# Column products of a graph-attention kernel: one fp32 table in place of two fp32r parts

## The reference

```
def _gat_conv(x, W, att_src, att_dst, bias, src, dst):      # twice, with W0 and W1
    xw = (x @ W).reshape(N, H, CPH)                          # H = 8 heads of 16 channels
    a_s = jnp.einsum('nhc,hc->nh', xw, att_src)
    a_d = jnp.einsum('nhc,hc->nh', xw, att_dst)
    e = jax.nn.leaky_relu(a_s[src] + a_d[dst], NEG)
    m = jax.ops.segment_max(e, dst, num_segments=N)
    p = jnp.exp(e - m[dst])
    s = jax.ops.segment_sum(p, dst, num_segments=N)
    return jax.ops.segment_sum(xw[src] * (p / s[dst])[:, :, None], dst, num_segments=N).reshape(N, H * CPH) + bias
...
x = x + _L0_gnn_ref(_layernorm(x, axis=-1), edge_index, ...)          # both convolutions side by side, + x, layernorm
x = x + _L0_ffn_ref(_layernorm(x, axis=-1)[None], ...)[0]             # 8 experts, 2 of them for each token
```

## Time and profile before

| what | us |
|---|---|
| time, median of 3 runs | 3142.97 |
| the profiled execution: span from first to last instruction | 3949.4 |
| busy in that span: TensorE / weight loads | 1918.5 / 1741.9 |
| busy: VectorE / ScalarE / GpSimd | 2043.1 / 1578.9 / 1927.4 |
| TensorE at L1299: 4080 MATMUL records | 953.7 busy |

### The profile page before, as it was taken

One profiled execution on the slowest core, in us unless ns is written; L12 is line 12 of the kernel. 1 busy time (PEld: TensorE's weight loads), 2 busy tenths in 40 slices (PEclk: granted clock), 3 DMA queues, 4 the chain that ended last, 5 costly groups with the idle time before them and its releaser, 6 DMA issues.

```text
span 3949.4 us, 38354 instructions
## 1 busy us (share of the span) xinstructions
PE 1918.5 (49%) x10116; PEld 1741.9 (44%) x10117; DVE 2043.1 (52%) x4266; ACT 1578.9 (40%) x2552; POOL 1927.4 (49%) x1920
## 2 busy tenths in 40 slices
PE   4500000134435354453544454545213489999998
PEld 2400000123425344353544453435213389999998
DVE  5465676625527355363554563545687544444443
ACT  4322223315536355453555554445323323333332
POOL 4467657645554555535555555465466612222222
PEclk8755555556767676676677776766655599999999
DMA  8244449313332333323333333233365622222222
GB/s 299 76 117 135 144 161 155 120 42 94 94 94 86 94 93 92 94 80 96 94 96 92 94 92 93 59 99 93 119 220 179 230 42 37 36 36 37 36 36 32
DMA packets 212942, 396.68 MB, mean 100 GB/s; under 512 B 76396, under 2 KB 164785, under 8 KB 206305
## 3 DMA queue, kind: packets, MB, share of 16 engines
q1 hardware_dynamic: 136049, 245.72, 18.4%
q0 software_dynamic: 75664, 149.21, 16.8%
q10 hardware_dynamic: 1120, 0.52, 0.0%
HBM read 203.53 MB, written 191.78 MB: 100 GB/s over the span
## 4 chain that ended last, share of the span: by engine, by line
PE 34%; issue 25%; DVE 16%; DVEq 10%; another core or an unknown queue 8%; ACT 4%; SPq 1%; POOL 1%; DMA 1%; POOLq 0%; ACTq 0%
PE ps L1299 13%; PE ps L1390 9%; PE ps L1396 9%; DVEq L1703 5%; DVE AR L1708 4%; PE ps L1270 1%; ACT onehot L1155 1%; ACT AR L1084 1%; DVEq L1709 1%; DVE AR L1773 1%; POOL AR L882 1%; DVE group_stats L1945 1%; ACT onehot L1159 1%; PE ps L1381 1%
## 5 line engine op out<-in xcount | busy, mean ns | idle before, releaser
L882 POOL DMA_INDIRECT AR<-tables,idx x1443 | 1377.0, 954 | 1095.5 <-DMA state<-AR 620.8
L1299 PE MATMUL ps<-table_parts,onehot 128*128 128x408 f32 (+1 forms) x4080 | 953.7, 388 | 1218.1 <-issue 752.5
L1299 PEld LDWEIGHTS ps<-table_parts,onehot 128*128 128x128 f32 x4080 | 861.9, 221 | 1309.9 <-issue 949.7
L1771 DVE TENSOR_SCALAR AR<-ps,tile_pick 128x136 f32<-128x136 f32 x120 | 35.4, 351 | 991.2 <-PE ps L1299 555.4
L1084 ACT COPY AR<-AR 128x1984 f32<-128x1984 f32 (+3 forms) x110 | 392.0, 3564 | 355.1 <-DVE AR L1708 195.6
L956 POOL DMA_INDIRECT out<-AR,idb x105 | 183.5, 1748 | 597.6 <-issue 560.1
L1708 DVE TENSOR_TENSOR_SCAN AR<-ps,AR 128x512 f32<-128x512 f32 x404 | 454.2, 1197 | 0.0
L1390 PEld LDWEIGHTS ps<-AR 128*128 128x128 f32 x3360 | 393.9, 193 | 6.6 <-DVE AR L2164 1.3
L1390 PE MATMUL ps<-AR 128*128 128x128 f32 x3360 | 394.5, 276 | 0.9 <-DVE AR L2164 0.9
L1701 DVE TENSOR_TENSOR AR<-AR,ps 128x3968 f32<-128x3968 f32 (+1 forms) x51 | 356.7, 6994 | 20.7 <-ACT AR L1103 13.4
L1101 ACT ACTIVATE ps<-AR 128x248 f32<-128x248 f32 (+1 forms) x51 | 19.2, 376 | 702.4 <-DVE AR L1688 411.4
(11 more groups left out here) (345 smaller groups left out, 2352.4 us busy)
## 6 DMA issues: line engine op xcount, KB each, us to landing
state<-AR SPq DMA_DIRECT2D x50, 2232.0 KB
AR<-tables,idx POOLq DMA_INDIRECT x1492
AR<-in_L_ffn_W SPq DMA_DIRECT2D x16, 1024.0 KB
AR<-placed SPq DMA_DIRECT2D x105, 130.0 KB, 2.0
adstart<-room SPq DMA_DIRECT2D x26, 496.0 KB
AR<-adstart SPq DMA_DIRECT2D x50, 248.0 KB
tables<-AR SPq DMA_DIRECT2D x49, 136.0 KB
room<-tables SPq DMA_DIRECT2D x14, 476.0 KB
```

Of the source, the lines that this page charges most:

```text
L882: pool.indirect_dma_start(out=G[s][:, j, 0:ROWT], out_offset=None, in_=table_rows, in_offset=bass.IndirectOffsetOnAxis(ap=idx[:, s, j:j + ...
L1299: return T.matmul(bank[:, 0:z], mark, table_parts[:, k, v * w:v * w + z], start=(a == 0 and k == 0), stop=(a == LEV - 1 and k == PARTS - 1))
```

## The change

The table is kept as plain fp32 in the area that x leaves, and each mark is multiplied with it once, as an fp32 product, so 17 products a column in place of 34. The transfer that reads it goes straight into that area, and so it is issued after all seven groups of x have been stored, when SP comes to batch 8. `split_table` and its semaphore go; ScalarE and TensorE wait for the transfer itself (`degrees_moved_then_table_loaded` at 48), and TensorE also for the second row of fix-ups (`fix_rows_ready` at 2), which reads a PSUM bank that the products write. One of the two buffers of edge codes moves to another place in the same area.

```
-PARTS = 2
-TABLE_AT = 5
-SPLIT_AT = 8
+TABLE_AT = 8
...
-        rounded = mybir.dt.float32r
         part_size = NT * ROWT
-        table_parts = nc.alloc_sbuf_tensor_at("table_parts", [P, PARTS, part_size], rounded, offset=arena_at + 4 * XO, align_bytes=4)
-        onehot = nc.alloc_sbuf_tensor_at("onehot", [P, LEV, PEC * P], rounded, offset=room_at, align_bytes=4)
-        at = FB + PARTS * part_size - NT * D
+        table = AR[:, XO:XO + part_size]
+        onehot = room[:, 0:LEV * PEC * P].rearrange("p (a c) -> p a c", a=LEV)
+        at = FB + 800
...
                     if b == TABLE_AT:
-                        sp.wait_ge(x_rows_stored, 16 * TABLE_AT)
+                        sp.wait_ge(x_rows_stored, 16 * NG)
...
-                        sp.dma_start(staging.rearrange("p (t r) -> p t r", r=ROWT), tab[0].rearrange("(t p) r -> p t r", p=P)).then_inc(degrees_moved_then_table_loaded, 16)
+                        sp.dma_start(table.rearrange("p (t r) -> p t r", r=ROWT), tab[0].rearrange("(t p) r -> p t r", p=P)).then_inc(degrees_moved_then_table_loaded, 16)
...
                 if i == 0:
-                    act.wait_ge(parts_ready, len(SPLITS))
+                    act.wait_ge(degrees_moved_then_table_loaded, 48)
...
-            def product(bank, mark, a, k):
+            def product(bank, mark, a):
...
-                return T.matmul(bank[:, 0:z], mark, table_parts[:, k, v * w:v * w + z], start=(a == 0 and k == 0), stop=(a == LEV - 1 and k == PARTS - 1))
+                return T.matmul(bank[:, 0:z], mark, table[:, v * w:v * w + z], start=(a == 0), stop=(a == LEV - 1))
...
                     for c in range(PEC):
-                        for k in range(PARTS):
-                            mm = product(column_banks[c], onehot[:, a, c * P:(c + 1) * P], a, k)
+                        mm = product(column_banks[c], onehot[:, a, c * P:(c + 1) * P], a)
...
-            pe.wait_ge(parts_ready, len(SPLITS))
+            pe.wait_ge(degrees_moved_then_table_loaded, 48)
+            pe.wait_ge(fix_rows_ready, 2)
...
-            def split_table(k):
...
-                for first, n in SPLITS[k]:
-                    a, z = first * ROWT, (first + n) * ROWT
-                    upper = room[:, part_size:part_size + n * ROWT]
-                    V.tensor_scalar(upper.bitcast(I32), staging[:, a:z].bitcast(I32), UPPER_BITS, None, ALU.bitwise_and)
-                    dd()
-                    V.tensor_copy(table_parts[:, 0, a:z], upper)
-                    last = V.tensor_tensor(table_parts[:, 1, a:z], staging[:, a:z], upper, ALU.subtract)
-                    dd()
-                last.then_inc(parts_ready, 1)
...
             def whole_batch(b, w=L, next_w=L):
-                if SPLIT_AT <= b < SPLIT_AT + len(SPLITS):
-                    split_table(b - SPLIT_AT)
```

More of the change, by code:

```diff
@@ L97 @@
 MIDDLE = float(LEV * P // 2)
-UPPER_BITS = -(1 << 12)
-SPLITS = (((0, 13), (13, 12)), ((25, 12), (37, 12)))
 LEVEL_ORDER = (0, LEV - 1, *range(1, LEV - 1))
@@ L296, in build @@
         columns_taken = sem("columns_taken")
-        parts_ready = sem("parts_ready")
         rows_copied = sem("rows_copied")
@@ L478, in build @@
         degree_rows = share_of.rearrange("p a b c t h -> p (a b c t h)")[0:NT, 0:P]
-        staging = room[:, 0:part_size]
         def repeats(w):
```

## The result

The changed kernel takes 3237.27 us (median of four runs, 3235.08 to 3240.13), the kernel before 3142.74 (four runs, 3141.74 to 3144.03). The medians differ by 94.5 us, a ratio of 1.0301; the ratio on record, formed from the fast runs with a 95% interval, is 1.0308 [1.0296, 1.0321]: slower. The forecast was 3303 us, in a range from 3195 to 3415; direction, mechanism and range held, and the size was 66 us too high.

A forecast was written before the change was run, and what follows sets the result against it. The prediction took GpSimd's gathers to bound the kernel before (34.3 us a batch) and TensorE's burst, pause and clock after (38.3 us): 40 x (38.3 - 34.3) = +160 us on 3143, 3303 us, range 3195 to 3415.

The forecast's parts named there:

- Mechanism: Batches 10 to 49: GpSimd's gathers set the pace before, TensorE's products at a mixed clock after; chance 0.56.
- The burst: TensorE's 102 records a batch at L1299: 33.6 us in fp32, where a free run took 20.76 us.
- The pause: TensorE's wait between bursts while VectorE empties three PSUM banks: 2.99 us, making the cycle 36.6 us at full clock.
- The clock: TensorE behind its pauses: after 9 of 17 it runs at 1.2 GHz and loses 3.2 us, 1.7 us a batch.
- P1: The changed kernel's batch, set by TensorE's burst, pause and clock: 38.3 us, ends 36.6 and 39.8.
- P0: The batch of a timed run before the change, set by GpSimd's gathers: 34.3 us, between 31.7 and 35.0.
- The lower bound: P0's lower end, 31.7 us: all 806.4 us of the profiled execution's excess lost in the 40 batches.
- rival 1: TensorE's clock holds through every pause: P1 36.6, +92 us, 3235 us (3205 to 3267); chance 0.08.
- rival 4: Gathers take 38.3 us or more a batch and hide TensorE's work: not slower, 3131 to 3149 us; chance 0.12.
- The split: Twelve VectorE instructions in two rounds (L1787 to L1790) go: costed at nothing, up to 12 us without the gathers' cover.
- The transfer: 3332 KB move from batch 5 to behind batch 8's store on SP's queue: cost nothing, if late at most some 10 us.
- The stalls: One-at-a-time products at TensorE, 752.5 us of waits before L1299: of the profiled execution alone, following records, not work.

The follow-up runs named there:

- second profile of before: The kernel before, unchanged, profiled once more: 3139.68 us, span 3137.9 us.
- half of the levels: The changed kernel with the column products of odd levels left out (9 of 17 levels stay): 3138.11 us, ratio 0.9981 to the kernel before.
- the spare bank: The changed kernel with a fourth PSUM bank: 3137.68 us, ratio 0.9977 to the kernel before; with the split's twelve VectorE instructions put back, 3140.17 us, 0.9999.
- two columns: 2 columns a batch on TensorE in place of 3: on the changed kernel 3184.52 us, ratio 1.0138; on the kernel before 3190.71 us, ratio 1.0156.
- the earlier trace: The profile of the kernel before that the prediction read; profiled execution 3949.4 us, median of the runs 3143.0 us.
- first profile of before: The kernel before, unchanged, in the profile that the prediction read: execution 3949.4 us, with stalls.
- a fourth column: The kernel before (two fp32r parts) with 4 columns a batch on TensorE in place of 3, the fourth in PSUM bank 0: 3090.71 us, ratio 0.9836.

## Why the prediction was right, and where its size was off

**Mechanism: right.** Gathers before, TensorE's cycle after. The second profile of before shows the gathers without a pause; half of the levels and the spare bank bring the batch back to 34.9 us and no further, two columns give 29 x 1.25 in both kernels. The signs named in the prediction's last part came too: 102 records a batch, VectorE waiting for the products, and GpSimd with 517.9 - 444.8 = 73 us of idle time ahead of gathers that isn't its own issue: 72.7 of it, in 28 waits, end with the stores that free a slot, where the second profile of before has 2.6 in one.

**The burst: right.** 33.84 us against 33.6, the price built from the expert stage. The Trainium skill, FP8 and Floating Point Precision, TensorE Precision Notes, gives a true fp32 product four passes through the array. The trace agrees for fp32: the burst bears out 340 ns for a record of 408 columns, two records a product, and 4 x 408 columns at one a cycle of 2.4 GHz, an estimate, are the same 680 ns. Doubling 20.76 would yet have given 41.5. The burst before was longer than its passes: its start was at the lower clock, and at the full clock a record took 183 ns, with weight loads busy for 14.87 of 15.00 us. In after, weight loads are busy for 773.8 us beside 1394.2 of products. So the likely pace of the burst before was one weight load a record and not the columns; no run moves the weight loads alone.

**The pause: right**, 2.99 us, as in the earlier trace rows. It is what turns a burst that would fit (34.0 a batch with the spare bank) into a cycle that doesn't.

**The clock: a mis-sized term.** I put it at 1.7 us a batch: 9 of 17 pauses, 3.2 us each. It measured 0.84 in the time, 1.02 in the records. The share was about right, 23 of 39 pauses where I had 9 of 17; but the clock mostly stays at the lower level for 2.9 us, not for 6.2 to 6.8, so that a burst mostly loses 35.27 - 33.84 = 1.4 us. Part of this was a misreading of the earlier trace rows: the four windows with a clock of 0.72 hold only 2 x 0.28 x 6.0 = 3.4 us at 1.2 GHz, and just the five near 0.50 stand for 6 us and more. With 1.7 us for the four and 3.2 for the five the term would have been 1.3. The rest was carried over from a kernel with bursts of 20.76 us to one with longer bursts. P1 was 37.67 us over the stage where I had 38.3; from burst to burst at TensorE it was (2107.46 - 670.40)/38 = 37.82, that is 33.84 + 2.99 + 0.99 for the clock.

**P0: a mis-sized term.** I took 34.3 us, between 31.7 and 35.0; it was 34.99, the upper bound. The lower bound had no mechanism: it only let all 806 us be lost in these batches. It was also miscounted: from one batch's largest instruction to another's, the 2072.9 us are 39 periods of 53.2 us and not 40 of 51.8, and the 422.1 us are 10 periods and not 9. By 39 the lower bound is 32.5, and a batch of 35.0 explains 708 of the 806 us in place of 673. The gathers at 1.25 us, in stalled and unstalled stretches alike, were a mechanism, and the batch of 29.3 us is no batch of 28 gathers. The first profile of before shows what it was:

```profile
1190.70:1220.10 29.40, 23.19 (x114) 22.40 (x113) 25.16 (x34) 24.46 (x29) 0.00 (x0) 0.88 0.09 28
```

```profile
1226.46 0.95 POOL L882 DMA_INDIRECT AR<-tables,idx  x1 [52.02 <-DMA state<-AR]
```

In the batch ahead of it, of 29.40 us, GpSimd does nothing. VectorE had stood for 61.17 us, until 1181.90, GpSimd had meanwhile filled all the slots it could and then stood 52.02 us until a store freed one. So VectorE ran these batches from slots filled earlier: 29.3 us is its own pace with a full stock, not that of a batch whose gathers have yet to be issued.

These two terms make 0.69 + 0.63 us a batch, 53 of the 66 us. Of the rest 6.8 us were gained outside the stage (5.2 + 1.6), 2.7 are the one period by which the stretch from batch 10 to batch 49 is shorter than the sum's 40, and 3.4 are the difference between what the profiled spans (97.9) and the medians (94.5) lose. The time lies at rival 1's 3235, but not for its reason: there the clock never fell, and P1 was 36.6. That the two agree is luck. Three small slips changed nothing: the lower ends 3205, 3333 and 3245 come to 2 us more by their own terms, and rival 4's 261 us to 265.

**The split: wrong at nothing.** I costed it at nothing because it comes "between gathers that set the pace", and at up to 12 us for the wait of ScalarE if that cover were gone. The cover itself was what it slows: the split lengthens the gathers by about 6.9 us. Taken out, it gave 5 to 7 us (the spare bank without and with it, ratios of 0.9977 and 0.9999 and gathers 5.2 us apart; the two-column kernels, 6.2 us apart in time and 6.9 in their gathers). The wait of ScalarE was only 5.15 us in the second profile and cost nothing that shows.

**The transfer: nothing, as said.** In after it is issued at 590.39 us, and ScalarE makes its first mark at 626.78 right behind its own work, with no wait for it. The stretch ahead of batch 10 is shorter by 5.2 us in after, against 5 to 7 for the split. VectorE's alternation of 10 us, in which such a cut falls, blurs a difference of that size, and no run moves the transfer alone.

**The stalls: half right.** That they belong to the profiled execution alone, on which the sum rested, held. That they "follow records, not work" did not: after has as many records and no stalls, and so has the kernel before in its second profile. What they follow stays open.

## What to carry to other kernels

Compare, for each engine, a whole cycle of a batch (its work, the pause in which its buffers are emptied, and what the clock takes behind that pause) with the bound that stands now: here a burst of 33.8 us would have fitted under 35.0 and lost by 3 us of pause, which a fourth bank hides. An instruction that lies beside the bounding engine's work isn't free for that reason: look whether the bounding engine's own instructions get longer beside it. And where the bound is one engine's even pace (28 x 1.25 us), simplifying another engine's work doesn't move it, while giving that engine a piece of the bound does: here a fourth column took 50 us off.

## What the runs showed of the hardware

**Some of VectorE's instructions in SBUF lengthen GpSimd's gathers.** 0.94 us becomes 1.38 to 2.55 beside the split's mask, copy and subtract. The Trainium skill, SBUF — State Buffer, SBUF: two separate sides, says that a DMA issued from GpSimd has its descriptors written by GpSimd, and that a VectorE instruction in a mode which takes the port pair shared by the two keeps it from writing them. The trace agrees in that the gathers beside these instructions, and not the one ahead of them at 0.94 us, are longer; which of the three kinds of instruction holds them most wasn't separated. Two instructions of one size in after's timeline suggest that the operands matter:

```profile
556.30 2.02 DVE L1880 TENSOR_TENSOR room<-room,ps 128x1792 f32<-128x1792 f32 x1 [6.18 <-ACT room L1123]
...
557.64 0.94 POOL L874 DMA_INDIRECT AR<-tables,idx  x1 [0.30 <-issue]
558.23 2.02 DVE L1881 TENSOR_TENSOR AR<-AR,bet 128x1792 f32<-128x1792 f32 x1
558.89 2.18 POOL L874 DMA_INDIRECT AR<-tables,idx  x1 [0.31 <-issue]
```

Beside the one that reads PSUM (`ps`) a gather takes 0.94 us; beside the one with both inputs in SBUF, 2.18.

**A pause of some 3 us brings the clock down in 23 of 39 cases**, mostly with some 2.9 us at 1.2 GHz behind it, and filling it with products that nobody reads keeps 2.4 GHz throughout: 33.7 us of 3237. The Trainium skill, TensorE: Matmul & The Clock Gate, Why this matters for your kernels, warns of longer idle gaps between bursts of products as what lets the throughput drop. The trace agrees for these 23 pauses; behind the other 16 nothing was lost.
